# Attention with exponentials of one bank each, loops written out, and an output tail that turns the weighed values to queries by heads

## The reference

```python
def _L0_xattn_ref(query, key, value, Wq, bq, Wk, bk, Wv, bv, Wo, bo, mask):
    ...
    scores = jnp.einsum('bhqd,bhkd->bhqk', q, k) / math.sqrt(D)
    scores = jnp.where(mask, scores, neg_inf)
    attention = jax.nn.softmax(scores, axis=-1)
    out = jnp.einsum('bhqk,bhkd->bhqd', attention, v)
    out = out.transpose(0, 2, 1, 3).reshape(Bt, St, E)
    return out @ Wo.T + bo
...
x = x + jnp.tanh(g_xattn[0]) * _L0_xattn_ref(_layernorm(x, axis=-1), ctx_1024, ctx_1024, ...)
x = x + jnp.tanh(g_ffn[0]) * _L0_ffn_ref(_layernorm(x, axis=-1), ...)
x = x + jnp.tanh(g_xattn[1]) * _L1_xattn_ref(_layernorm(x, axis=-1), ctx_1024, ctx_1024, ctxb_2048x8, ...)
x = x + jnp.tanh(g_ffn[1]) * _L1_ffn_ref(_layernorm(x, axis=-1), ...)
```

## Time and profile before

| | us |
|---|---|
| runs, median of 3 (lowest to highest) | 1180.16 (1178.17 to 1180.94) |
| the profiled execution, its own time | 1175.95 |
| its span, first to last instruction | 1174.2 |
| TensorE busy (PE) | 1022.6, 87% |
| VectorE busy (DVE) | 853.9, 73% |
| ScalarE busy (ACT) | 543.2, 46% |
| GpSimd busy (POOL) | 349.4, 30% |
| mean granted TensorE clock, share of full speed | 0.911 |

### The profile page before, as it was taken

How to read it: one execution, slowest core, us unless ns; L and a number is a source line. 1 busy time by engine, 2 the same in 40 slices (tenths; PEclk the granted TensorE clock), 3 DMA queues, 4 the chain that set the end, 5 groups by cost and what they waited for, 6 DMA issues and landing times.

```text
span 1174.2 us, 27964 instructions
## 1 busy us (share of the span) xinstructions
PE 1022.6 (87%) x9788; PEld 715.6 (61%) x9788; DVE 853.9 (73%) x1943; ACT 543.2 (46%) x810; POOL 349.4 (30%) x278
## 2 busy tenths in 40 slices
PE   4889999799979999958999689999899899861997
PEld 2356666566656666647888446666566566541886
DVE  7977777667767776667999787778678578540896
ACT  2033534343434445625666315555555455640664
POOL 6522121212121201005777441242142241000674
PEclk8589999999989999968999959999899899975899
DMA  7531303030303040008554323414304304004662
GB/s 182 98 68 36 77 27 78 28 77 27 77 28 77 2 104 1 2 11 235 165 166 137 66 77 81 99 31 100 78 27 91 80 11 104 3 1 66 180 166 69
DMA packets 48235, 89.05 MB, mean 76 GB/s; under 512 B 21170, under 2 KB 31446, under 8 KB 48118
## 3 DMA queue, kind: packets, MB, share of 16 engines
q1 hardware_dynamic: 48118, 87.42, 30.6%
HBM read 47.70 MB, written 1.75 MB: 42 GB/s over the span
## 4 chain that ended last, share of the span: by engine, by line
PE 71%; DVE 12%; issue 8%; ACT 2%; POOL 1%; DVEq 0%; ACTq 0%; POOLq 0%
PE pm L1129 16%; PE po L1177 14%; PE ps L1156 12%; PE ps L1294 8%; PE ps L1159 6%; PE pm L1294 4%; PE pc L1086 4%; PE pc L1103 3%; DVE mx_part L420 2%; DVE qsel L528 2%; DVE negm L430 2%; PE pc L1201 1%; PE pc L1195 1%; DVE qst L438 1%; POOL tmpf L775 1%
## 5 line engine op out<-in xcount | busy, mean ns | idle before, releaser
L851 ACT ACTIVATE probs<-ps 121x800 f32<-121x800 f32 (+1 forms) x384 | 321.3, 838 | 339.9 <-PE ps L1159 216.3
L1129 PE MATMUL pm<-khi,qbd 128*100 128x482 f32 (+5 forms) x653 | 317.9, 498 | 12.8 <-DVE mx_part L417 9.7
L417 DVE CUSTOM_DVE_ANT_0 junk<-pm,negq 100x482 bf16<-100x482 f32 (+1 forms) x360 | 229.5, 654 | 76.4 <-PE pm L1129 58.8
L1156 PE MATMUL ps<-qst,kst 128*121 128x400 f32 (+1 forms) x768 | 263.8, 409 | 19.7 <-issue 13.8
L420 DVE TENSOR_REDUCE mx_part<-pm 128x1 f32<-128x482 f32 (+3 forms) x293 | 183.6, 650 | 49.7 <-PE pm L1129 49.6
L1177 PE MATMUL po<-probs,vaug 121*32 121x100 f32 x6144 | 216.0, 259 | 3.9 <-ACT oraw L879 3.6
L1177 PEld LDWEIGHTS po<-probs,vaug 121*32 121x32 f32 x6144 | 129.8, 111 | 118.3 <-issue 105.0
L1156 PEld LDWEIGHTS ps<-qst,kst 128*121 128x121 f32 (+1 forms) x768 | 142.3, 189 | 60.6 <-issue 40.9
L1129 PEld LDWEIGHTS pm<-khi,qbd 128*100 128x100 f32 (+2 forms) x653 | 115.2, 178 | 89.2 <-issue 36.6
L1294 PE MATMUL ps<-qsel,qst 128*128 128x400 f32 x660 | 140.6, 365 | 1.1 <-DVE qst L520 1.1
L775 POOL TENSOR_TENSOR tmpf<-vaug,wb 128x400 f32<-128x400 f32 x55 | 67.1, 1220 | 220.3 <-DMA wb<-routing 160.6
(11 more groups left out here) (176 smaller groups left out, 1109.8 us busy)
## 6 DMA issues: line engine op xcount, KB each, us to landing
kst<-khi SPq DMA_DIRECT2D x128, 180.5 KB, 3.8
wb<-routing SPq DMA_DIRECT2D x66, 200.0 KB, 3.5
ctxT<-in_ctxT SPq DMA_DIRECT2D x16, 722.0 KB, 4.4
kst<-klo SPq DMA_DIRECT2D x64, 180.5 KB, 3.9
wts<-in_experts SPq DMA_DIRECT2D x55, 192.0 KB, 3.4
wb<-routing SPq DMA_DIRECT2D x22, 400.0 KB, 4.0
qsel<-qhi SPq DMA_DIRECT2D x16, 100.0 KB, 2.4
routing<-vaug SPq DMA_DIRECT2D x1, 1100.0 KB
```

The lines of the kernel that those rows point to most:

```text
L417: ins = nc.vector.tensor_tensor_reduce(junk[:, k % 2, 0:w], max_bank(b, k)[0:S, 0:w], negq[:, lo:lo + w], 1.0, -3e38, ALU.add, ALU.max, mx ...
L851: nc.scalar.activation(probs[t % 2][0:r, 2 * u * GQ:2 * (u + 1) * GQ].rearrange("p (g q) -> p g q", q=GQ), ps[0:r, 2 * u:2 * u + 2, 0:GQ], ...
L1129: nc.tensor.matmul(max_bank(b, k)[0:rows, 0:w], qbd[:, first:first + rows], khi[:, lo:lo + w], start=True, stop=True).then_inc(s["chunk_re ...
L1156: mm = nc.tensor.matmul(ps[0:r, g, 0:GQ], kst[par][:, g, t * KEY_TILE:t * KEY_TILE + r], qst[par][:, g * GQ:(g + 1) * GQ], start=True, sto ...
```

## The change

It has three parts. Each bank of scores is signalled by itself, and `exp_group` takes one bank of 400 columns. Every `Fori` of every engine, in attention and experts, becomes a Python loop, so that all turns stand in the program one behind the other. And the tail goes another way: in slot 3 four transposes turn `oraw` so that the 100 queries lie on the partitions and the heads (32 columns each) along the free dimension; VectorE takes one reciprocal of the 16 denominators and one product of 128 columns; in slot 5 a transpose turns the result back (`turn_back`), VectorE copies it (`take_back`), and in slot 7 one matmul projects it with an unpadded `wo`. `den_sel` and the padding of `wo` go, and the constants by which the maxima are spread change. Cut to its core (the other `Fori` lines of ScalarE, VectorE, GpSimd, SyncE and of the experts change in the same way, and the calls of the exponentials follow their new form):

```diff
@@ -77,14 +77,13 @@
-DEN_SLOT, OUT_SLOT = 3, 7
-RECIPROCAL_SLOTS = {3: [0], 4: [1], 5: [2], 6: [3]}
+DEN_SLOT, BACK_SLOT, OUT_SLOT = 3, 5, 7
...
-SCORES_TIME, WEIGH_TIME, K_TIME, V_TIME, DEN_TIME, OUT_TIME, TURN_TIME = (34, 17), 30, 80, 100, 67, 100, 10
+SCORES_TIME, WEIGH_TIME, K_TIME, V_TIME, DEN_TIME, BACK_TIME, OUT_TIME, TURN_TIME = (34, 17), 30, 80, 100, 40, 10, 25, 10
@@ -92,8 +91,8 @@
-TAIL = G + 3
-OUT_TAKEN = G + 1
+TAIL = 4
+OUT_TAKEN = 2
...
@@ -152,7 +150,7 @@
         wv = [sb(f"wv{l}", [128, 128]) for l in range(2)]
-        wo = [sb(f"wo{l}", [128, G, 128]) for l in range(2)]
+        wo = [sb(f"wo{l}", [128, 128]) for l in range(2)]
         bq = [sb(f"bq{l}", [128, 1]) for l in range(2)]
...
@@ -441,20 +440,24 @@
-                def reciprocals(b, g):
-                    cols = slice(g * S, (g + 1) * S)
-
-                    dve.wait_ge(s["tail_ready"], 2 * b + 1)
-                    nc.vector.reciprocal(rden[:, cols], pc[:, cols]).then_inc(s["tail_step"], 1)
-
                 def normalise(b):
-                    dve.wait_ge(s["tail_step"], b * TAIL + G)
-                    dve.wait_ge(s["oraw_ready"], b + 1)
-                    nc.vector.tensor_tensor(onorm[:], oraw[:], rden[:], ALU.mult).then_inc(s["onorm_ready"], 1)
+
+                    turned = pc[0:S, :].rearrange("q (h e) -> q h e", e=32)
+                    dve.wait_ge(s["tail_ready"], 3 * b + 1)
+                    nc.vector.reciprocal(rden[:].unsqueeze(2), turned[:, :, DH:DH + 1]).then_inc(s["tail_step"], 1)
+                    dve.wait_ge(s["tail_step"], b * TAIL + 1)
+                    nc.vector.tensor_tensor(onorm[:].rearrange("q (h d) -> q h d", d=DH), turned[:, :, 0:DH],
+                                            rden[:].unsqueeze(2).broadcast_to([S, H, DH]), ALU.mult)\
+                        .then_inc(s["onorm_ready"], 1)
+
+                def take_back(b):
+
+                    dve.wait_ge(s["tail_ready"], 3 * b + 2)
+                    nc.vector.tensor_copy(onormT[:], pc[:, 0:S]).then_inc(s["onormT_ready"], 1)
...
-                    dve.wait_ge(s["tail_ready"], 2 * b + 2)
+                    dve.wait_ge(s["tail_ready"], 3 * b + 3)
                     nc.vector.tensor_tensor(t2[0:S, 0:D], pc[0:S, 0:D], bo[l][0:S, :], ALU.add)\
@@ -469,9 +472,10 @@
                         k_low(b + 1, t)
-                    if tail:
-                        for g in RECIPROCAL_SLOTS.get(t, []):
-                            reciprocals(b - 1, g)
+                    if tail and t == DEN_SLOT:
+                        normalise(b - 1)
+                    if tail and t == BACK_SLOT:
+                        take_back(b - 1)
@@ -482,8 +486,6 @@
                                 beside(b, t, main, tail)
-                            if tail and t == max(RECIPROCAL_SLOTS) and i == 1:
-                                normalise(b - 1)
                         if tail and t == OUT_SLOT:
@@ -492,14 +494,13 @@
                     energy_gates()
-                with dve.Fori(0, (B - 2) // 2) as i:
+                for i in range((B - 2) // 2):
                     for k in range(2):
...
                 layer_norm(2 * l + 1, "a")
-                for g in range(G):
-                    reciprocals(B - 2, g)
                 normalise(B - 2)
+                take_back(B - 2)
@@ -508,9 +509,8 @@
                 add_out(B - 2)
-                for g in range(G):
-                    reciprocals(B - 1, g)
                 normalise(B - 1)
+                take_back(B - 1)
                 add_out(B - 1)
...
@@ -842,14 +842,13 @@
-                def exp_half(b, t, u):
+                def exp_group(b, t, g):
                     r = rows_of(t)
-                    act.wait_ge(s["scores_ready"], b * (2 * KEY_TILES) + (2 * t + u + 1))
+                    act.wait_ge(s["scores_ready"], b * (G * KEY_TILES) + (G * t + g + 1))
...
                         act.wait_ge(s["pv_done"], b * KEY_TILES + (t - 1))
-                    nc.scalar.activation(probs[t % 2][0:r, 2 * u * GQ:2 * (u + 1) * GQ].rearrange("p (g q) -> p g q", q=GQ),
-                                         ps[0:r, 2 * u:2 * u + 2, 0:GQ], ACT.Exp,
+                    nc.scalar.activation(probs[t % 2][0:r, g * GQ:(g + 1) * GQ], ps[0:r, g, 0:GQ], ACT.Exp,
                                          scale=SCALE).then_inc(s["probs_ready"], 1)
...
@@ -905,7 +906,7 @@
                     step(nc.scalar.activation(egate[:], egate[:], ACT.Exp, scale=-1.0), "energy_exp")
-                with act.Fori(0, (B - 2) // 2) as i:
+                for i in range((B - 2) // 2):
                     for k in range(2):
...
@@ -1138,7 +1139,7 @@
                 def scores(b, t, g, par):
-                    r, u = rows_of(t), g // 2
+                    r = rows_of(t)
                     if t == 0 and g == 0:
@@ -1149,10 +1150,9 @@
                         pe.wait_ge(s["negm_ready"], b * writes + (g + 1 if g < G - 1 else writes))
-                    if g % 2 == 0:
-                        if not (isinstance(b, int) and b == 0 and t == 0):
-
-                            pe.wait_ge(s["probs_ready"], b * (2 * KEY_TILES) + (2 * t + u - 1))
+                    if not (isinstance(b, int) and b == 0 and t == 0):
+
+                        pe.wait_ge(s["probs_ready"], b * (G * KEY_TILES) + (G * t + g - (G - 1)))
                     mm = nc.tensor.matmul(ps[0:r, g, 0:GQ], kst[par][:, g, t * KEY_TILE:t * KEY_TILE + r],
@@ -1160,12 +1160,11 @@
                                               start=False, stop=True)
-                    if g % 2 == 1:
-                        mm.then_inc(s["scores_ready"], 1)
+                    mm.then_inc(s["scores_ready"], 1)
...
                     r = rows_of(t)
-                    pe.wait_ge(s["probs_ready"], b * (2 * KEY_TILES) + (2 * t + u + 1))
+                    pe.wait_ge(s["probs_ready"], b * (G * KEY_TILES) + (G * t + 2 * u + 2))
                     if t == 0 and u == 0:
@@ -1192,15 +1191,18 @@
                     pe.wait_ge(s["oraw_ready"], b + 1)
-                    nc.tensor.matmul(pc[:, 0:GQ], den_sel[:], oraw[:], start=True, stop=True)\
+                    for g in range(G):
+                        mm = nc.tensor.transpose(pc[0:S, g * 128:(g + 1) * 128], oraw[:, g * S:(g + 1) * S], ident[:])
+                    mm.then_inc(s["tail_ready"], 1)
+
+                def turn_back(b):
+                    pe.wait_ge(s["onorm_ready"], b + 1)
+                    nc.tensor.transpose(pc[:, 0:S], onorm[:], ident[0:S, 0:S]).then_inc(s["tail_ready"], 1)
+
+                def project(b):
+                    pe.wait_ge(s["onormT_ready"], b + 1)
+                    nc.tensor.matmul(pc[0:S, 0:D], onormT[:], wo[l][:], start=True, stop=True)\
                         .then_inc(s["tail_ready"], 1)
-
-                def project(b):
-                    pe.wait_ge(s["onorm_ready"], b + 1)
-                    for g in range(G):
-                        mm = nc.tensor.matmul(pc[0:S, 0:D], onorm[:, g * S:(g + 1) * S], wo[l][:, g, :],
-                                              start=(g == 0), stop=(g == G - 1))
-                    mm.then_inc(s["tail_ready"], 1)
@@ -1210,10 +1212,11 @@
                         spreads = after and t == DEN_SLOT
+                        turns_back = after and t == BACK_SLOT
                         projects_out = after and t == OUT_SLOT
...
                         whole = (main * G * SCORES_TIME[l] + weighs * 2 * WEIGH_TIME + projects_k * K_TIME
-                                 + projects_v * V_TIME + spreads * DEN_TIME + projects_out * OUT_TIME
+                                 + projects_v * V_TIME + spreads * DEN_TIME + turns_back * BACK_TIME + projects_out * OUT_TIME
                                  + turns_maxima * TURN_TIME)
@@ -1248,6 +1251,9 @@
                             maxima(DEN_TIME)
+                        if turns_back:
+                            turn_back(b - 1)
+                            maxima(BACK_TIME)
                         if projects_out:
@@ -1275,13 +1281,14 @@
                 slots(0, True, False, True, 0)
-                with pe.Fori(0, (B - 2) // 2) as i:
+                for i in range((B - 2) // 2):
                     for k in range(2):
...
                 den(B - 1, False)
+                turn_back(B - 1)
                 project(B - 1)
...
@@ -1556,9 +1562,7 @@
         a[f"wq{l}"], a[f"wk{l}"], a[f"wv{l}"] = w["q"], w["k"], w["v"]
-        wo = np.zeros((J, 32, G, D), f)
-        wo[:, 0:DH] = w["o"].reshape(G, J, DH, D).transpose(1, 2, 0, 3)
-        a[f"wo{l}"] = wo.reshape(128, G, D)
+        a[f"wo{l}"] = w["o"]
         a[f"bq{l}"], a[f"bk{l}"] = b["q"][:, None], b["k"][:, None]
```

33 lines of the change are left out of this document (17 added, 16 removed).

## The result

The changed kernel takes 1133.13 us (median of 4 runs, 1132.53 to 1136.61) against 1180.55 before in the same comparison: a ratio of 0.960 (95% interval 0.958 to 0.963), 47.4 us less. The forecast was 1146.8 with a range of 1134 to 1164. The direction was right, and so were the mechanisms of the loops and the tail; the sign of the exponentials was wrong. In the runs beside the experiments, the kernel before had medians of 1179.0 to 1180.0; differences between versions that were measured beside different runs of it can be off by 1 to 2 us for that alone.

The account below looks back on a forecast made before the run. TensorE's stream was taken to bound attention and to pace the experts. Terms -19.2 - 10 - 6.5 + 0.7 + 1.6 = -33.4 us took the profiled 1175.95 to 1142.5; 4.2 for the median gave 1146.8 us, range 1134 to 1164.

Parts of the forecast that it names:

- loops written out: Attention loops of both layers: removing two jumps back per layer, with idle time and slow clock after, saves 19.2 us; expert loops nothing.
- tail in 14 batches, layer ends, `add_out`: New tail: 10 us saved inside 14 batches, 6.5 us at the ends of the layers, 0.7 us taken back in layer 0.
- exponentials: ScalarE: 400 instead of 800 columns adds 63 us of work, mostly hidden under TensorE; +1.6 us on the time.
- the three undisturbed batches: Layer 0's attention batches without a jump back, mean 55.99 us, against which jumps were costed at 4.41 and 4.34 us.
- The bound of 21: Upper bound in us of the saving from removing attention's jumps, taken against the shortest batch of the same layer.
- The tail in the middle: TensorE in slots 3, 5 and 7 of 14 batches: 1.58 us removed, some 0.87 added, 0.71 saved each, 10 us.
- Rival 1: VectorE, pacing the maxima in slots 8 to 10, takes up the tail's saving: 1156.8 us, chance 0.12.
- The layer ends: Bare tail after each layer's last batch: new steps take about 3.05 us; gain 3.5 + 3.0 = 6.5 us, all on the path.
- the late `add_out(B - 2)`: Layer 0's end: VectorE's last piece before the final tail starts behind routing, so TensorE's slot 7 gain is lost, +0.7 us.
- catching up: Layer 1's last batch: ScalarE recovers more slowly after the square root's table loads with 400-column exponentials, +0.5 us.
- rival 2: Straight code is fetched as slowly as a jump's target, or the expert stages now stall: 1166 us, chance 0.08.
- rival 3: Exponentials on in-order ScalarE become the bound and all 63 us come onto the path: 1210 us, chance 0.05.

## Why the prediction was right, and where it was wrong

| term | forecast | measured | from |
|---|---|---|---|
| loops written out | -19.2 | -25.7 | loops alone, medians |
| tail in 14 batches, layer ends, `add_out` | -15.8 | -18.5 | changed kernel with the old tail |
| exponentials | +1.6 | -2.4 | changed kernel with 800 columns |
| sum | -33.4 | -46.6 | (the whole change: -47.4) |

The parts add up to within 0.8 us. That is closer than the runs can tell, since the second and third were measured beside other runs of the kernel before (1179.0) than the whole (1180.55); nothing large is left between them.

**The loops: right mechanism, wrong baseline.** This is the term that missed by most, 25.7 us against 19.2. The step that failed is "the mean of the three undisturbed batches is 55.99": I charged only the batches that begin with a jump and took the others for what straight code gives. By the traces, batches 1 to 6 of layer 0 took 342.7 us before and 327.5 with loops written out, -15.3 where 8.75 were forecast. Of it 3.7 us lie in the four batches without a jump. The two with one gained 11.6 against 54.6, the mean of the straight code. In layer 1 it is 265.7 against 253.0, -12.7 instead of 10.45, and 1.5 of it in batches without a jump. Two things were wrong with the baseline. There are four such batches in layer 0 and not three: the one of 54.03 us, the only one at clock 1.00, was left out, and with it the mean is 55.50. And all four carry the loops' costs, 0.2 us each in layer 0 and 0.4 in layer 1 at the same clock. The remaining gain of layer 0's batches without a jump is that fewer of them hold the low clock, and why is not shown. The bound of 21 came from the shortest batch among those shown, 55.46; with 54.03 it would have been 23.6, and still too low.

It was wrong too that the other engines jump "behind TensorE's wait, so their share is in these numbers". TensorE's loop written out alone gave 19.6 us, so for its jumps the 19.2 had about the right size, in part by luck, as its baseline was too long. The loops of the other four engines, put at nothing by that sentence, cost 5.3 us more. That the expert loops cost nothing was right.

**The tail in the middle: right sum of TensorE, one item missing.** The half slot with the transposes came to 2.20 us, as forecast, and a batch lost 3 matmul instructions. At the same clock a batch lost 1.0 us in layer 0 and 0.44 in layer 1, 0.71 in the mean, which is the forecast, though neither layer has it by itself. By the medians less is left of it: the version with the old constants is 5.4 us slower, so the tail alone holds 13.1 of the 18.5. Between the traces of the old tail and of the new one with the old constants the layer ends hold 7.2 of these (6.62 to 3.35 and 6.51 to 2.60), so about 6 remain for 14 batches, 0.4 each; the two batches of layer 0 that fell from clock 1.00 to 0.97 between these traces cost 3 us. The item missing is the constants, which "change" in the diff and no more. I gave them no price, and the sum is too low by their 5.4 us, of which 2 can be seen in the batches at the same clock. Rival 1 (VectorE takes up the saving) is not seen in layer 0. In layer 1 TensorE's busy time fell by 0.57 us a batch and the batch by 0.44, so no more than 0.13 us each was taken up.

**The layer ends: right.** 3.05 us forecast; 3.75 in layer 0, with the 0.7 for the late `add_out(B - 2)` that was costed apart, and 2.60 in layer 1. Forecast 5.8 in all, measured 6.3 between the traces before and after (2.77 and 3.50).

**The exponentials: wrong sign.** One takes 503 ns, 501 were forecast, and in layer 1's last batch a pair just fits: the rhythm stayed at 1.04 us. But "two are 1002, so a pair grows by 164 ns" was too much: two that follow each other take 0.90 us together in the timeline, 0.06 more than one of 800 columns, and the busy time of all exponentials grew from 321.3 to 347.8 us, by 26.5 instead of 63. What failed is "bank-wise release gives TensorE nothing, since it hardly waits for ScalarE now". Where ScalarE comes late from the table loads TensorE does wait, and there one bank is ready 0.45 us sooner. That catching up "gets slower" was the wrong half of that thought. Most of the saving of 2.4 to 3.0 us has no place in the traces, so its cause is open. The rule of the Trainium skill ("ScalarE: Activation LUTs", "What ACT_TABLE_LOAD costs") that neighbours overlap by about 93 ns was nearer than my row, which took no overlap: the timeline shows 0.11 us (2 x 0.503 - 0.90). The time did not hang on it.

**The rivals.** Straight code brought no stalls (rival 2): TensorE's weight loads before a scores matmul were idle with "issue" for 20.7 us in all, 40.9 before. ScalarE, busy for 25 of 41.6 us, became no bound (rival 3).

**The range.** Three terms erred in one direction, by 6.5, 2.7 and 4.0 us. I had let the range go 17 us to the slow side, for the rivals, and 13 to the fast side, where it had to hold the loops term, whose upper bound was taken from batches that were themselves disturbed, and the constants, which had no term at all.

## What to carry to other kernels

The batches of a loop that do not jump are no picture of the code without the loop: let the upper bound of such a term be open, or write out the loop of one engine and look. Compare batches at the same granted clock, and take all of them into the baseline: here one of four was left out, and a stretch of low clock (1.5 us) is larger than what the tail saves in a batch. An instruction on the critical path that takes ten times as long as its shape (16 columns, 1.82 us) is worth a look at what another engine does in the same microsecond; here one added wait on GpSimd gave 10 us, a fifth of what the whole change gave. Constants that share out work are a term of the change: after a step gets shorter they must be set anew; the version with the old ones was 5 us slower. A load that is issued later can move its wait on to another unit: see whether the whole stretch became shorter, and not only the unit that had stalled.

## What the runs showed of the hardware

- VectorE's negation of 100x16 from SBUF to SBUF did not end until GpSimd's product did: 1.82 us beside it, 0.18 without. The reduction of 100x48 ran beside the product in 0.20 us. The Trainium skill ("SBUF — State Buffer", "🔬 SBUF: two separate sides") has the pair of ports that these engines share as an exclusive lock for a whole instruction, taken by some forms of VectorE's instructions and not by others; the runs agree with it.
- A border where TensorE idled 1.84 us was followed, in five batches of six, by a stretch at the lower clock (1.2 GHz); with 0.20 us of idle time it stayed at 2.4 GHz in five batches of seven. At the same clock the shorter wait gave 1.16 us a batch (52.62 to 51.46), and such a stretch costs 1.5 (54.12 against 52.62).
- A jump of TensorE over a body of two batches costs about 5 us in all (19.6 us for four), one over four expert units nothing that can be measured (76.15 against 76.12 us for all units of layer 1).
- The loops of engines that do not bound the kernel cost too: with TensorE's loop already written out, those of the four others took 0.6 us from each batch of layer 1 (42.73 to 42.14).
